# First MoE of a two-layer gated attention and MoE kernel: 13 full expert tiles, listed from the counts of 20 token tiles, run between the last routers' steps; the rest are listed at the end

## What is computed

```python
x = x + jnp.tanh(g_xattn[0]) * _L0_xattn_ref(_layernorm(x, axis=-1), ctx_1024, ctx_1024, mask_BxSxS2_ik1, ...)
x = x + jnp.tanh(g_ffn[0]) * _L0_ffn_ref(_layernorm(x, axis=-1), ...)
x = x + jnp.tanh(g_xattn[1]) * _L1_xattn_ref(_layernorm(x, axis=-1), ctx_1024, ctx_1024, ..., 16)
x = x + jnp.tanh(g_ffn[1]) * _L1_ffn_ref(_layernorm(x, axis=-1), ...)
```

```python
top1 = jnp.argmax(jnp.einsum('bld,ed->ble', x, Wg), axis=-1)
for e in range(8):
    h = jax.nn.gelu(jnp.einsum('bld,dh->blh', x, W1[e]) + b1[e], approximate=False)   # 128 -> 512
    y = jnp.einsum('blh,hd->bld', h, W2[e]) + b2[e]                                   # 512 -> 128
    out = jnp.where((top1 == e)[..., None], y, out)
```

## Time and profile before

| | us |
|---|---|
| timed runs, median of 3 | 594.4 |
| timed runs, lowest and highest | 590.74 and 594.51 |
| profiled execution, device time | 589.1 |
| its span, first to last instruction | 587.2 |

### The profile page before, as it was taken

The page is one execution under the profiler, slowest core; times in us unless marked ns, Lnnn a source line. Parts: engine busy times, 40 slices in busy tenths (PEclk is TensorE's granted clock), DMA queues, the critical chain, the costliest instruction groups (busy, mean ns, idle before and its releaser), DMA issues.

```text
span 587.2 us, 17304 instructions
## 1 busy us (share of the span) xinstructions
PE 501.4 (85%) x6026; PEld 373.5 (64%) x6026; DVE 379.6 (65%) x1150; ACT 319.7 (54%) x763; POOL 272.6 (46%) x325
## 2 busy tenths in 40 slices
PE   2899998999889826999996688998998888897887
PEld 1466776776657715999994365776676657654444
DVE  6669789787654651444442587898998678453355
ACT  3455655567534423566662554666667365575554
POOL 2534344552625360677777543434444243443455
PEclk9999999999965855999998598999999788588999
DMA  6128423320011211344444404100000000000112
GB/s 182 46 61 179 120 79 89 104 78 29 20 42 33 65 45 38 45 63 65 63 60 68 122 3 109 38 29 3 20 12 2 2 2 3 1 2 1 37 42 69
DMA packets 50356, 30.39 MB, mean 52 GB/s; under 512 B 12128, under 2 KB 46688, under 8 KB 50272
## 3 DMA queue, kind: packets, MB, share of 16 engines
q1 hardware_dynamic: 32224, 17.23, 11.1%
q0 software_dynamic: 6640, 4.67, 6.1%
q10 hardware_dynamic: 11408, 7.38, 4.5%
HBM read 19.41 MB, written 9.85 MB: 50 GB/s over the span
## 4 chain that ended last, share of the span: by engine, by line
PE 66%; DVE 11%; issue 9%; ACT 7%; DMA 2%; POOL 2%; SPq 1%; ACTq 1%; another core or an unknown queue 1%; DVEq 0%; POOLq 0%
PE T_ps L832 8%; PE A_ps L845 8%; PE f_H_ps L1052 8%; PE S_ps L821 6%; PE f_Y_ps L1061 6%; DVE maxes L568 4%; PE Q_ps L738 3%; PE Q_ps L802 3%; PE S_ps L815 3%; PE X_ps L861 3%; PE m_H_ps L1268 2%; PE Q_ps L727 2%; PE m_T_ps L1308 2%; PE m_X_ps L1295 2%; PE m_X_ps L1251 2%
## 5 line engine op out<-in xcount | busy, mean ns | idle before, releaser
L568 DVE TENSOR_REDUCE maxes<-S_ps 128x8 f32<-128x512 f32 x128 | 87.7, 685 | 55.4 <-PE S_ps L821 55.3
L395 POOL TENSOR_TENSOR k_blk<-kT,col_a 128x512 f32<-128x512 f32 x64 | 67.6, 1067 | 87.9 <-ACT kT L456 57.1
L498 ACT ACTIVATE probT<-T_ps 128x512 f32<-128x512 f32 x128 | 76.1, 594 | 54.0 <-PE T_ps L832 49.7
L832 PE MATMUL T_ps<-col_a,prob 128*128 128x128 f32 x512 | 87.6, 297 | 10.2 <-DVE prob L576 5.9
L832 PEld LDWEIGHTS T_ps<-col_a,prob 128*128 128x128 f32 x512 | 60.1, 149 | 49.9 <-issue 36.9
L576 DVE TENSOR_TENSOR prob<-S_ps,maxes 128x512 f32<-128x512 f32 x128 | 88.5, 692 | 4.4
L1013 POOL DMA_INDIRECT x_mid<-f_out,f_rows x39 | 60.5, 1552 | 38.3 <-DVE f_out L986 38.0
L845 PEld LDWEIGHTS A_ps<-v_blk,probT 128*64 128x64 f32 x2048 | 67.3, 142 | 11.4 <-issue 11.2
L845 PE MATMUL A_ps<-v_blk,probT 128*64 128x18 f32 x2048 | 73.7, 215 | 0.0
L977 DVE TENSOR_TENSOR f_hid<-f_H_ps,f_b 128x512 f32<-128x512 f32 x39 | 27.0, 692 | 50.1 <-PE f_Y_ps L1061 39.7
L821 PE MATMUL S_ps<-k_blk,qT 32*64 32x256 f32 x1024 | 48.2, 434 | 4.7 <-DVE prob L576 4.2
(11 more groups left out here) (187 smaller groups left out, 929.8 us busy)
## 6 DMA issues: line engine op xcount, KB each, us to landing
f_w<-in_W ACTq DMA_DIRECT2D x16, 256.0 KB
ctxT<-in_ctxT SPq DMA_DIRECT2D x12, 256.0 KB, 3.0
f_rows<-sorted_rows SPq DMA_DIRECT2D x39, 64.5 KB
out<-m_final SPq DMA_DIRECT2D x32, 64.0 KB, 1.5
x_all<-in_x SPq DMA_DIRECT2D x6, 256.0 KB, 5.7
x_mid<-x_all SPq DMA_DIRECT2D x6, 256.0 KB
x_all<-x_mid SPq DMA_DIRECT2D x6, 256.0 KB, 3.6
ctxT<-in_ctxT SPq DMA_DIRECT2D x8, 128.0 KB, 2.3
```

Source lines behind the costliest of these rows:

```text
L395: nc.gpsimd.tensor_tensor(k_blk[:, t % 2, :, :, :], kT[:, g.at(R), t - g.first, :].rearrange("p (b k) -> p b k", b=2).unsqueeze(2).to_broa ...
L498: nc.scalar.activation(probT[:, t % 2, 4 * h:4 * h + 4, :], T_ps[:, :, :], ACT.Exp, scale=SCALE).then_inc(probT_ready, 1)
L568: nc.vector.tensor_reduce(maxes[:, t % 2, h, :, :], half_of(h), X, ALU.max).then_inc(max_ready, 1)
L832: last = nc.tensor.transpose(T_ps[:, j, :], pair, ident[:, :])
```

## The change

The counts of the first 20 token tiles (groups 0 to 5) are enough to be sure of 13 row tiles that are full, whatever the routing: 20 x 128 rows less at most 127 for each of the 8 experts. These 13 are listed from the counts of group 5 (`count_full`, `list_full`), and each engine's part of them is put into its list of attention steps: the list at steps 28 to 30.5, the loads at 30.5, and the tiles in slots at 31.5, 32, 33 ... 39, 39.6, 40, 40.5 and 41 (`SLOTS_AT`). In slot n PE turns tile n, runs `up` of n - 1 and `down` of n - 3, and POOL's add of n - 4 follows. The 26 other tiles are listed from all counts at step 39 and 39.7 and run behind. Regions are now filled from their first row, a tile starts at its expert's next row, and so pads are wanted behind each expert's last row and not before its first: the early pad DMA is gone, and eight DMAs of 3 x 128 rows each (`pad_ends`) are issued by SP from rows known once group 8 is counted. Group 9's scatters wait for all eight (`ends_padded`). The rings of loaded rows grow from 8 to 16. For ACT the order within a slot becomes Gelu, weights, `turn_out`. Groups 3 and 4 are ranked two steps sooner than before, group 6 one step later, and the last scatters' due times are one step sooner. `kept` and `scattered` become two semaphores or sets each, one for the first 20 tiles. The core of the diff:

```diff
+FULL_GROUPS = 6
+FULL_FROM = 20
+FULL_TILES = -(-(FULL_FROM * P - E0 * (P - 1)) // P)
+SIZES = (2, 2, 4, 4, 4, 4, 4, 4, 2, 2)
+LAST_PADS = 1 + SIZES[-1]
...
+FULL_AT = 28
+REST_AT = 39
+SLOTS_AT = (31.5, 32, 33, 34, 35, 36, 37, 38, 39, 39.6, 40, 40.5, 41)
+FULL_SLOTS = len(SLOTS_AT)
...
-def settled(skew, steady, short=LAST_GROUPS):
-    return lambda g: g.last + (steady if g.own < short else lag(g) + skew)
+def settled(skew, steady, short, later=()):
+    return lambda g: g.last + (steady if g.own < short else lag(g) + skew + (g.own in later))
...
-        short = LAST_GROUPS
+        short = 3 if masked else LAST_GROUPS
+        later = (3, 4, 6) if masked else ()
...
+                if g.own == NG - 1:
+                    pool.wait_ge(r["ends_padded"], 16 * E0)
                 pool.indirect_dma_start(r["sorted"], bass.IndirectOffsetOnAxis(ap=row[:, t:t + 1], axis=0),
-                                        r_xn[:, t, :], None).then_inc(scattered[t % 4], 16)
+                                        r_xn[:, t, :], None).then_inc(scattered[t >= FULL_FROM][t % 4], 16)
...
-                steps += [(scatter, tiles, lambda t: settled(8, 13, short)(GROUP_OF[t]) + (t - GROUP_OF[t].first) // 2)]
+                steps += [(scatter, tiles, lambda t: settled(8 if GROUP_OF[t].own < 7 else 7, 13, short, later)(GROUP_OF[t]) + (t - GROUP_OF[t].first) // 2)]
...
-    RINGS = 8
+    RINGS = 16
...
+    def placed(steps):
+        return [(step, range(FULL_SLOTS - skew), lambda t, skew=skew: slot_at(t + skew)) for step, skew in steps]
+
     def staggered(steps):
-        for n in range(MAX_TILES + max(skew for _, skew in steps)):
+        for n in range(FULL_SLOTS, MAX_TILES + max(skew for _, skew in steps)):
...
+        def count_full(_):
+            dve.wait_ge(r["casts"], 7)
+            dve.wait_ge(done["counted"], FULL_GROUPS)
+            vec.tensor_tensor(over[:, :, :], start[:, :].unsqueeze(2).to_broadcast([P, E0, NT]), r["full"][:, :, :], ALU.is_ge).then_inc(full_chain, 1)
+            dve.wait_ge(full_chain, 1)
+            vec.tensor_reduce(tiles[:, :], over[:, :, :], X, ALU.add).then_inc(full_chain, 1)
+            dve.wait_ge(full_chain, 2)
+            vec.tensor_scalar(jump[:, :], tiles[:, :], -float(P), float(REGION), ALU.mult, ALU.add).then_inc(full_chain, 1)
+
+        def list_full(_):
+            prefix(full_chain, 3)
+            passing(full_chain, 5)
+            vec.tensor_scalar(pair[:, 1:2], n_passed[:, :], float(E0 - 1), None, ALU.min).then_inc(listed, 1)
+            vec.tensor_scalar(pair[:, 0:1], jumped[:, :], r["row_at"][:, 0:1], None, ALU.add).then_inc(listed, 1)
...
+        def pad_from(_):
+            dve.wait_ge(done["counted"], NG - 1)
+            vec.tensor_copy(pad_at[:, :], start[0:1, :]).then_inc(pads_known, 1)
+
+        def list_rest(_):
+            dve.wait_ge(done["counted"], NG)
+            dve.wait_ge(taken_chain, 5)
+            vec.tensor_tensor(over[:, :, :], start[:, :].unsqueeze(2).to_broadcast([P, E0, NT]), r["reach"][:, :, :], ALU.is_gt).then_inc(chain, 1)
+            dve.wait_ge(chain, 1)
+            vec.tensor_reduce(left[:, :], over[:, :, :], X, ALU.add).then_inc(chain, 1)
+            dve.wait_ge(chain, 2)
+            vec.tensor_tensor(tiles[:, :], left[:, :], taken[:, 0:E0], ALU.subtract).then_inc(chain, 1)
+            vec.tensor_tensor(skipped[:, :], taken[:, 1:E0 + 1], left[:, :], ALU.subtract).then_inc(chain, 1)
+            dve.wait_ge(chain, 4)
+            vec.tensor_scalar(jump[:, :], skipped[:, :], float(P), float(REGION), ALU.mult, ALU.add).then_inc(chain, 1)
+            prefix(chain, 5)
+            passing(chain, 7)
+            dve.wait_ge(listed_turned, 1)
+            vec.tensor_scalar(pair[:, 1:2], n_passed[:, :], float(E0 - 1), None, ALU.min).then_inc(listed, 1)
+            vec.scalar_tensor_tensor(pair[:, 0:1], jumped[:, :], r["row_at"][:, 0:1], first_row[:, 0:1], ALU.add, ALU.add).then_inc(listed, 1)
...
+        def note(part):
+            def step(_):
+                dve.wait_ge(listed_turned, part + 1)
+                vec.tensor_copy(tabs[part][:, :], list_ps).then_inc(table, 1)
+                dve.wait_ge(table, part + 1)
+            return step
+
+        return [(count_full, once, lambda _: FULL_AT), (list_full, once, lambda _: FULL_AT + 1), (note(0), once, lambda _: FULL_AT + 2.5),
+                (take_full, once, lambda _: FULL_AT + 2), (pad_from, once, lambda _: REST_AT - 2), (list_rest, once, lambda _: REST_AT), (note(1), once, lambda _: REST_AT + 0.7)] + placed(tile_vector(dve))
...
+    def load(sp):
+        def step(t):
+            if t == 0:
+                sp.wait_ge(table, 1)
+                for s in done["scattered"][0]:
+                    sp.wait_ge(s, 16 * FULL_FROM // 4)
+            if t == FULL_TILES:
+                sp.wait_ge(table, 2)
+                sp.wait_ge(r["padded"], 16)
+                for s in done["scattered"][1]:
+                    sp.wait_ge(s, 16 * (NT - FULL_FROM) // 4)
+            row = sp.value_load(entry(0, t), min_val=0, max_val=ROWS - P)
...
+        def pad_ends(_):
+            sp.wait_ge(pads_known, 1)
+            sp.wait_ge(r["pads_ready"], 1)
+            for e in range(E0):
+                row = sp.value_load(pad_at[0:1, e:e + 1], min_val=0, max_val=E0 * REGION - LAST_PADS * P)
+                sp.dma_start(r["sorted"][bass.ds(row, LAST_PADS * P), :].rearrange("(n p) d -> p n d", p=P),
+                             r["pads"][:, e:e + 1, :].to_broadcast([P, LAST_PADS, RW])).then_inc(r["ends_padded"], 16)
+
+        return [(load(sp), range(FULL_TILES), lambda t: FULL_AT + 2.5), (pad_ends, once, lambda _: REST_AT - 2)]
...
+    def tile_gpsimd(pool):
+        def send(t):
+            if t == 0:
+                pool.wait_ge(done["kept"][0], 16 * FULL_GROUPS)
+            if t == FULL_TILES:
+                pool.wait_ge(done["kept"][1], 16 * (NG - FULL_GROUPS))
...
+        return [(send, 4)]
...
+        return [(gelu, 3), (weights, 0), (turn_out, 0)]
...
+    def tile_tensor(eng):
         def turn(t):
+            if t == 0:
+                eng.wait_ge(done["shifted"], 2 * NT)
...
+        def turn_list(part):
+            def step(_):
+                eng.wait_ge(listed, 2 * part + 2)
+                done["x_bank"]["x"].take(table, part + 1)
+                pe.transpose(list_ps, pair[:, :], r["ident"][:, :]).then_inc(listed_turned, 1)
+            return step
+
+        return [(turn_list(0), once, lambda _: FULL_AT + 2.5), (turn_list(1), once, lambda _: REST_AT + 0.7)] + placed(tile_tensor(eng))
...
-                sp.dma_start(r0["sorted"][0:E0 * REGION, :].rearrange("(e p) d -> p e d", p=REGION)[0:P, :, :], r0["pads"][:, 0:E0, :]).then_inc(r0["padded"], 16)
```

More of the change, by code:

```diff
@@ L285, in attention @@
     rows_ready = sem("rows_ready")
-    scattered = [sem(f"scattered{k}") for k in range(4)]
+    scattered = [[sem(f"scattered{part}{k}") for k in range(4)] for part in ("_full", "_rest")]
     top_ready = sem("top_ready")
@@ L441, in gpsimd @@
             blocks = gpsimd_steps(pool)
-            steps = [(blocks, tiles if masked else tiles[2:], shift(-2)), (norm, groups, head(-10)), (r_norm, groups, settled(3, 6, short))]
+            steps = [(blocks, tiles if masked else tiles[2:], shift(-2)), (norm, groups, head(-10)), (r_norm, groups, settled(3, 6, short, later))]
             if masked:
-                steps += [(scatter, tiles, lambda t: settled(8, 13, short)(GROUP_OF[t]) + (t - GROUP_OF[t].first) // 2)]
+                steps += [(scatter, tiles, lambda t: settled(8 if GROUP_OF[t].own < 7 else 7, 13, short, later)(GROUP_OF[t]) + (t - GROUP_OF[t].first) // 2)]
             else:
-                steps += [(gaps, groups, settled(7, 11, short))]
+                steps += [(gaps, groups, settled(7, 11, short, later))]
             steps += [(add_bias, groups, head(-4))]
@@ L902, in experts0 @@
     jumped = sb("jumped", [P, 1])
+    taken_to = sb("taken_to", [P, E0])
+    taken = sb("taken", [P, E0 + 1])
+    left = sb("left", [P, E0])
+    skipped = sb("skipped", [P, E0])
+    first_row = sb("first_row", [P, 1])
     pair = sb("pair", [P, 2])
-    tab = sb("tab", [2, P], I32)
+    tabs = [sb(f"tab{k}", [2, P], I32) for k in range(2)]
+    pad_at = sb("pad_at", [1, E0], I32)
     rows = sb("rows", [P, RINGS, RW])
@@ L987, in finish @@
                               b2[:, bass.ds(e, 1), :].rearrange("p a c -> p (a c)"), ALU.add).then_inc(y_out, 1)
-        dve.wait_ge(r["scaled"], 1)
-        dve.wait_ge(done["kept"], 16 * NG)
-        staggered([(bias, 1), (finish, 3)])
-    def sync(sp):
-        sp.wait_ge(table, 1)
-        sp.wait_ge(padded, 16 * 2)
-        for s in done["scattered"]:
-            sp.wait_ge(s, 16 * NT // 4)
-        for t in range(MAX_TILES):
-            row = sp.value_load(tab[0:1, t:t + 1], min_val=0, max_val=ROWS - P)
+        return [(bias, 1), (finish, 3)]
@@ L1002, in sync, with drain_sync @@
```

(21 more changed lines are left out.)

163 lines of the change are left out of this document (93 added, 70 removed).

## The result

| us | before | after |
|---|---|---|
| median | 592.57 | 576.00 |
| lowest and highest | 590.27 and 594.51 | 572.25 and 577.66 |
| profiled execution, device time | 589.1 | 575.04 |
| its span | 587.2 | 573.0 |

The ratio is 0.973, 95% interval 0.969 to 0.978: 2.7% faster, about 16 us. I had 585.0, and 579.0 as the lower end. The direction was right; the size was not, and, as the experiments show, neither was the reason.

What follows compares the result with a forecast made beforehand. TensorE's time was taken as the bound: tile 13 at 241.4, plus 2.6, 55.0 and 7.3, put the last add at 306.3 instead of 316.0. Median 594.4 - 9.7 = 584.7, written 585.0; range 579 to 595.5.

Steps and rivals of the forecast that it cites:

- The start: End of layer 0's attention: tile 0 can be turned at about 199.8 us, and the clock falls at 201.3.
- The drain: Tiles between the last router steps: each step its router part plus 2.12 us, TensorE ready for tile 13 at 235.8.
- Gelu's table load: In the drain at step 34: ACT loads Gelu's table (1.28 us), and TensorE loses 1.1 us before second matmuls.
- Rival (c): Pads' wait or chained drain steps run longer and take most of the gain: 591.0, or 594 to 597; chance 0.17.
- The pads: Eight pad DMAs after group 8's count: first at 221.7 us, 13.0 us taken, down at 234.7, holding POOL's last scatters.
- the stand: Before tile 13, TensorE stands 5.6 us behind pads and last scatters, until tile 13 is turned at 241.4.
- 26 slots of 2.115: From tile 13 to the last tile's first matmuls: 55.0 us, plus 2.6 for the low clock, ending at 299.0.
- POOL isn't the bound: Layer 0's last adds: POOL alone could finish at 237.2 + 34 x 1.85 = 300.1, before the forecast 306.3.
- (a): Clock doesn't fall in the drain: 3.3 us earlier, 2.6 more without a later fall, 581.7 to 579.1; chance 0.15.
- (b): Low clock in the drain lasts 20.5 us instead of 6.7: 6.9 us later, 591.9; chance 0.22.
- (d): Slower than before: low clock from 201.3 past 235, 34.1 us, makes it 13.7 us later, 598.7; chance 0.08.

Runs made afterwards that it cites:

- change_again: The changed kernel, unaltered, timed and profiled a second time on another chip; ratio to the kernel before 0.973.
- early_pads: The changed kernel with pads written at fixed rows at the kernel's start, the eight pad DMAs of the drain gone; ratio to the kernel before 0.981.
- late_pads: The changed kernel with pads written behind the last counts, one tile per expert, only tile 13's load waiting for them; ratio to the kernel before 0.976.
- old_due_times: The changed kernel with the router's due times of groups 3, 4 and 6 as before; ratio to the kernel before 0.978.
- old_act_order: The changed kernel with ACT's old order in a slot (weights, turn_out of the tile before, Gelu); ratio to the kernel before 1.001.
- pads_aside: The changed kernel with pads written early at fixed rows, plus the drain's eight pad DMAs into an array nobody reads; ratio to the kernel before 0.979.
- new_order_in_drain: The changed kernel with ACT's new order only in the drain's slots, the old order for tiles 13 to 38; ratio to the kernel before 0.986.
- new_order_behind: The changed kernel with ACT's old order in the drain and the new one for tiles 13 to 38; ratio to the kernel before 0.992.

## Why the prediction was wrong

**The start: right.** Tile 0 was forecast at 199.8 and is turned at 198.14; the clock falls at 199.8 (forecast 201.3).

**The drain: wrong in size.** I counted the router part plus 2.12 for a slot, 36.0 us for the thirteen, with 1.1 us of waiting in all. They take 43.0, with 8.7 us of waiting; step 12's matmuls end at 241.2 instead of 235.8. 2.0 us of that are behind Gelu's table load, where I had the 1.1. The other three waits are for a Gelu that stands behind a router's step in ACT's queue, 1.9 us behind a normalisation at 215.75 and 4.8 us behind copies at 224.66 and 229.22, which had themselves stood for something unnamed (see Open). Rival (c) named it, "steps chained over ACT and DVE", and I gave it no part of the sum.

**The pads: nearly right.** First DMA at 221.62 (221.7), issues until 231.7, POOL's scatter at 237.81 (234.7 was the landing that I took; my bounds were 11.3 and 19.0 us from the first issue, it is 16.2). Tile 13 at 244.34 (241.4), the stand 3.2 us instead of 5.6, since TensorE was late itself.

**Behind tile 13: the failed step, "26 slots of 2.115".** I took the pace of the kernel before over to one whose ACT order was different; the new order appears nowhere in my sum. From tile 13 to the last first matmuls it is 50.8 us, not 57.6: 1.90 a slot and 1.4 for the low clock at the start. The sign of it was in the earlier trace rows: from 235 to 310 I read PE's 75.00 of 75 us as no wait, but the weight loads beside it (PEld) fill only 68.50. Those 6.5 us are the 0.19 us a slot for which they wait for ACT's copy; in after PEld is full too, 50.00 of 50. The ring of 16, which I had under nothing too, is what lets this pace hold. That pair is worth 2.1% of the 2.7% alone, and without the order the rest is worth nothing.

**"POOL isn't the bound": false once the slot is 1.90.** My 237.2 + 34 x 1.85 = 300.1 was the right sum. POOL started at 240.39 instead, because of the pads, and so sets the last add at 303.69, 8.5 us behind the last first matmuls instead of 7.3.

So errors of both signs met: tile 13 2.9 late, 6.8 less behind it, 1.2 more at the end, 306.3 forecast and 303.69 measured. These 2.6 us, 1.9 of layer 1, and 4.3 from carrying an execution 5.3 under its median over to the median (that of after lies 1.0 under its own) make the 9 us between 585.0 and 576.0. The last add agreed within 2.6 us for wrong reasons: of my 9.7 us for tiles in the drain the runs show at most 3 (103.8 to 105.4 against 104.5 and 106.8), and 13 come from two edits that I had costed at nothing. The 1.9 us of layer 1 are within its scatter, so that share is luck.

**Rivals.** (a), (b) and (d) turned on the clock: it was 0.87 from 200 to 225, low in short pieces, so neither always full nor 20.5 us low. (c), tiles in the drain without time saved, was true of its part.

**Open.** In the drain of after ACT, DVE and TensorE stand together for about 3 us where the profile names no releaser ("remote"):

```profile
224.66 0.17 ACT L544 COPY l_logits<-Q_ps 128x16 f32<-128x16 f32 x1 [4.28 <-remote]
229.22 0.18 ACT L550 COPY rank_now<-Q_ps 128x24 f32<-128x24 f32 x1 [3.14 <-remote]
```

Such waits are in the drains of the change, change_again, early_pads, late_pads and old_due_times (in old_act_order one of 2.11 us), and not in those of pads_aside, new_order_in_drain and new_order_behind, which ran on another chip, nor with the tiles behind the drain. What causes them isn't known. They cost tile 13 little: new_order_in_drain has the change's own drain without them, and turns it 44.9 us behind the last `attend`, against 46.0 and 44.8. There step 12 is done sooner, but TensorE then stands 5.0 us for the rows of tile 13, because the chain from the first pad DMA to tile 13 is hardly shorter (21.2 us against 22.7). pads_aside, without these waits and without the wait for the pads, came to tile 13 after 41.8 us, where I had forecast 43.0 for the change.

## What to carry to other kernels

Price every edit of a diff against the slot that repeats most often: a wait of 0.19 us in the row of a steady slot, times 39, and a ring deep enough for the new pace outweighed a redesign of the drain. Look for that wait in the row of the weight loads too: a PE row that is full does not say that there is none. Look for the circle that sets the pace (buffer free, copy, copy, matmul), and when one engine gets faster ask which ring, sized for the old pace, runs dry next. Work put between dependent small steps fills the busy share, but also delays those steps and whatever is chained to them.

## What the runs showed of the hardware

TensorE reached a slot of 1.90 us (0.27 for the turn, 1.06 and 1.06 for the matmuls, overlapping) with no wait over 50 us at the full clock. POOL's indirect adds came no faster than one in 1.86 us (1.55 and 0.30 of issue), so it is the next bound, 0.04 us under TensorE. Eight DMAs of pads to DRAM, 1548 KB in runs of 516 bytes, were issued over 10.1 us and held the next scatter until 16.2 us after the first issue. And with 1548 KB more of pads near 50 us TensorE was busy 53.3 us instead of 57.5 from 40 to 100 us.
